# A decoder layer's first attention, with relative positions: groups over four query tiles, bias applied as a factor, operand rows made by 0/1 matmuls

## What is computed

```python
idx = jnp.arange(s)
dist = jnp.clip(idx[None, :] - idx[:, None], -R, R) + R      # R = 64
pe_k = rel_emb_k[dist]
pe_v = rel_emb_v[dist]
q, k, v = (qkv[0], qkv[1], qkv[2])
q = q / jnp.sqrt(jnp.asarray(hd, x.dtype))
score = jnp.einsum('bhqd,bhkd->bhqk', q, k) + jnp.einsum('bhqd,qkd->bhqk', q, pe_k)
attn = jax.nn.softmax(score, axis=-1)
ctx = jnp.einsum('bhqk,bhkd->bhqd', attn, v) + jnp.einsum('bhqk,qkd->bhqd', attn, pe_v)
return ctx @ W_out + b_out
```

## Time and profile before

| | us |
|---|---|
| median of 3 runs | 554.8 (551.67 to 556.12) |
| the profiled execution | 553.47 |
| its span, first to last instruction | 551.6 |
| TensorE busy | 445.8 |
| VectorE busy | 343.0 |
| ScalarE busy | 264.6 |
| GpSimd busy | 56.4 |
| mean granted TensorE clock | 0.849 |

### The profile page before, as it was taken

One profiled execution on the slowest core, in us unless ns is written; L12 is line 12 of the kernel. 1 busy time (PEld: TensorE's weight loads), 2 busy tenths in 40 slices (PEclk: granted clock), 3 DMA queues, 4 the chain that ended last, 5 costly groups with the idle time before them and its releaser, 6 DMA issues.

```text
span 551.6 us, 17721 instructions
## 1 busy us (share of the span) xinstructions
PE 445.8 (81%) x7898; PEld 277.8 (50%) x7898; DVE 343.0 (62%) x703; ACT 264.6 (48%) x547; POOL 56.4 (10%) x71
## 2 busy tenths in 40 slices
PE   0504777999999999899999757398899999878995
PEld 0300524777787877778988646242222222263452
DVE  3698465887666566465222206679688989165586
ACT  1700213555555464645656623135887878655211
POOL 1793000000000000000000007006200000000011
PEclk9855555999989797978897957588899999999999
DMA  8999993000000000000000150101800000000000
GB/s 159 165 206 310 163 295 61 2 4 4 4 4 4 4 4 4 4 4 4 6 4 5 41 163 4 36 1 37 193 1 2 2 0 1 2 1 0 1 15 24
DMA packets 18437, 26.81 MB, mean 49 GB/s; under 512 B 2688, under 2 KB 15256, under 8 KB 17832
## 3 DMA queue, kind: packets, MB, share of 16 engines
q1 hardware_dynamic: 16841, 19.38, 15.8%
q0 software_dynamic: 1520, 6.30, 4.9%
HBM read 16.68 MB, written 8.44 MB: 46 GB/s over the span
## 4 chain that ended last, share of the span: by engine, by line
PE 61%; DVE 13%; DMA 11%; ACT 8%; issue 4%; SPq 1%; POOLq 0%; POOL 0%; ACTq 0%; DVEq 0%
PE ps L1013 7%; PE ps L1050 7%; PE ps L1030 6%; PE ps L1001 6%; PE ps L1262 5%; PE ps L1312 5%; PE ps L980 4%; PE ps L1249 4%; DMA scr<-ctxT 4%; PE ps L1061 3%; DMA q_op<-neg_mT 2%; ACT crel L507 2%; DVE m_qk L849 2%; PE ps L1231 2%; DMA scr<-rel_v 2%
## 5 line engine op out<-in xcount | busy, mean ns | idle before, releaser
L700 DVE TENSOR_REDUCE m_qk<-ps 128x1 f32<-128x512 f32 x128 | 85.0, 687 | 47.8 <-PE ps L980 46.1
L980 PE MATMUL ps<-k_op,q_op 112*128 112x512 bf16 x128 | 60.1, 478 | 31.8 <-DMA k_op<-scr 23.3
L849 DVE TENSOR_REDUCE m_qk<-ps 128x2 f32<-128x1024 f32 x64 | 75.0, 1218 | 10.7 <-PE ps L1231 10.6
L487 ACT ACTIVATE band<-ps 128x512 f32<-128x512 f32 x64 | 38.2, 596 | 83.4 <-PE ps L1013 83.4
L1013 PE MATMUL ps<-q_op,rel_k 112*128 112x32 bf16 x1024 | 69.9, 235 | 5.8 <-DMA rel_k<-scr_rel 4.3
L611 ACT ACTIVATE band<-ps 128x512 f32<-128x512 f32 x128 | 66.9, 593 | 13.7 <-PE ps L1249 13.7
L1013 PEld LDWEIGHTS ps<-q_op,rel_k 112*128 112x128 bf16 x1024 | 63.4, 117 | 15.2 <-DMA q_op<-scr 4.8
L743 DVE TENSOR_TENSOR band<-ps,band 128x512 f32<-128x512 f32 x64 | 43.8, 684 | 36.3 <-PE ps L1030 29.5
L1030 PE MATMUL ps<-q_op,k_op 113*128 113x64 bf16 x1024 | 56.6, 204 | 4.2 <-issue 1.9
L1030 PEld LDWEIGHTS ps<-q_op,k_op 113*128 113x128 bf16 x1024 | 46.3, 105 | 18.0 <-issue 7.6
L524 ACT ACTIVATE p_out<-ps 128x512 f32<-128x512 f32 x64 | 38.2, 597 | 29.2 <-PE ps L1050 28.5
(11 more groups left out here) (202 smaller groups left out, 607.4 us busy)
## 6 DMA issues: line engine op xcount, KB each, us to landing
q_op<-in_zeros SPq DMA_DIRECT2D x2, 1024.0 KB
scr<-band SPq DMA_DIRECT2D x2, 768.0 KB, 10.8
scr<-rel_v SPq DMA_DIRECT2D x2, 768.0 KB, 10.1
...
```

Of the source, the lines that this page charges most:

```text
L700: dve.tensor_reduce(m_qk[:, tt, 8 * e + p:8 * e + p + 1], ps[:, bank, :], AX_X, ALU.max).then_inc(sm["m_done"], 1)
L849: dve.tensor_reduce(m_qk[:, IT * b + it, 2 * p:2 * p + 2], ps[:, 2 * (su % 2):2 * (su % 2) + 2, :], AX_X, ALU.max).then_inc(sm["rmax_done" ...
L980: i = pe.matmul(ps[:, bank, :], q_op[0:PR, e, p, tt * P:tt * P + P], k_op[0:PR, 0, p, b * S:b * S + S], start=True, stop=True)
```

## The change

The first attention is written anew; the rest stays, apart from where tiles lie in memory.

- A group u is one strip of 32 queries out of each of the four query tiles of a batch (8 groups of 128 queries). q_op's columns are permuted so that a group's are contiguous. For one offset x in the strip the window of relative keys is the same in all four tiles.
- Bias: the matmul for one x takes 8 pairs x 4 (or 3) tiles as columns, over 49 rows, once for even and once for odd heads at rows 0 and 64. ScalarE exponentiates it into eb; scores are exponentiated by themselves; GpSimd multiplies the near part of the exponentials by exp(bias). The near keys of a query are its own tile and the one on the nearer side.
- Far keys no longer have operands of their own. v_sb has seven blocks of 9 columns, so that 27 weight columns carry the values of one class in one of three places, the far classes in rows 9 to 26 of each 32. fin multiplies those by exp(far bias minus the relative maximum) and adds the three.
- Two separate maxima, of the relative scores and of q·k, enter as operand rows 48 and 49.
- Operand rows come from three bf16 parts by matmuls with a 0/1 matrix loaded from DRAM (sel), over strips of 32 rows, in place of the way through scr. In the rotary attention too sel is loaded rather than written by GpSimd, and its picks take 32 rows.
- The order is a list, relative_plan: step t, a rank in the step, a kind. Each engine runs through it. Banks 4 to 6 are a ring for all that ScalarE empties, banks 0 to 3 two pairs for VectorE, bank 7 holds PV.
- The transposes and the division move from the finish into each group (fin, back).
- Constants of the rotary attention and w_conv are loaded at the start, the MLP's weights after the last product with exp(bias).

Instructions of TensorE in the first attention, by source (a float32 matmul counted once):

| | before | after |
|---|---|---|
| bias | 1,024 of 112 rows, 32 columns | 1,024 of 49 rows, 32 or 24 columns |
| scores | 1,024 of 113 rows, 64 columns | 512 of 50 rows, 128 columns |
| maxima | 128 of 112 rows, 512 columns | 128 of 48 rows, 512 columns |
| PV | 1,024, 9 weight columns, 64 columns | 1,152, 27 weight columns, 32 to 96 columns |
| relative values | 1,024, 32 columns | 1,024, 32 or 24 columns |
| their addition | 256 of 8 rows, 64 columns | 512 of 128 rows, 32 columns |
| picks | none | 99 of 16 or 32 rows, 512 columns |

The core of the diff:

```diff
+GROUP = 11
+QK_BANKS = ((2, 3), (7, 0))
+V_BANKS = (1, 7)
+PAIR_BANKS = (slice(2, 4), slice(0, 2))
+PICK_ORDER = ((0, 2), (1, 3), (4, 6), (5, 7))
...
+def side(u):
+    return -1 if u % IT < IT // 2 else 1
+def second(u):
+    return (1 if side(u) < 0 else 0), IT - 1
+def regions(u, jt):
+    lo, hi = (jt, jt + 1) if side(u) < 0 else (jt - 1, jt)
+    parts = [(max(lo, 0), min(hi, IT - 1), 0), (0, lo - 1, 2), (hi + 1, IT - 1, 1)]
+    return [(a, z - a + 1, c) for a, z, c in parts if z >= a]
...
+def relative_plan():
+    plan = [(-1, 0, "relk", 0, 0)]
+    for n, k in enumerate((0, 1, 2)):
+        plan.append((-1, 1 + n, "pick", 0, k))
+    for k, t in ((3, 0), (4, 1), (5, 2), (6, 3), (7, 4)):
+        plan.append((t, 3, "pick", 0, k))
+    plan.append((2, 4, "v1", 0, 0))
+    for k in range(8):
+        plan.append((5 + k, 3, "pick", 1, k))
+    plan.append((12, 3.5, "zero", 0, 0))
+    for u in range(NT):
+        t = GROUP * u
+        plan += [(t + j, 1, "rel", u, j) for j in range(3)]
+        plan += [(t + 3 + p, 1, "max", u, p) for p in range(PAIRS)]
+        plan += [(t + 5, 4, "rel_rows", u, 0), (t + 6, 4, "factors", u, 0), (t + 13, 4, "qk_rows", u, 0)]
+        plan += [(t + 8 + q, 5, "bias", u, q) for q in range(4)]
+        plan += [(t + 16 + GROUP * p // PAIRS, 2, "scores", u, p) for p in range(PAIRS)]
+        plan += [(t + 24 + 2 * g, 6, "pv", u, g) for g in range(4)]
+        plan += [(t + 25 + 5 * f, 7, "crel", u, f) for f in range(2)]
+        plan += [(t + 27 + 5 * f, 8, "add", u, f) for f in range(2)]
+        plan += [(t + 33, 9, "ctx", u, 0), (t + 34, 1.5, "fin", u, 0), (t + 37, 9, "back", u, 0)]
+    return [(kind, u, n) for _, _, kind, u, n in sorted(plan, key=lambda x: x[:2])]
...
+of_act = {"relk": 1, "pick": 2, "rel_rows": 1, "qk_rows": 1, "bias": 2, "scores": 2, "crel": 1, "back": 1}
...
+sp.dma_start(ident[:, :], t["ident"]).then_inc(sm["ld_id"], 16)
+sp.dma_start(w_qkv[:, :], t["w_qkv"]).then_inc(sm["ld_wq"], 16)
+sp.dma_start(cols[:, :], t["cols"]).then_inc(sm["ld_wq"], 16)
+sp.dma_start(sel[:, :, :, :], t["sel"]).then_inc(sm["ld_sel"], 16)
+for u in range(2):
+    sp.dma_start(relk_f[HD * u:HD * u + HD, :], t["relk_ext"]).then_inc(sm["ld_rel"], 16)
+sp.dma_start(rows[:, :, :], bass.AP(t["rows"].tensor, 0, [[0, P], [1, 7 * D]])).then_inc(sm["ld_w"], 16)
+sp.dma_start(rel_v[:, :], bass.AP(t["relv_ext"].tensor, 0, [[HD, P], [1, 384 * HD]])
+             ).then_inc(sm["relv_ready"], 16)
+sp.dma_start(w_out[:, :], t["w_out"]).then_inc(sm["ld_w"], 16)
...
-zeros = lambda r, n: bass.AP(t["zeros"].tensor, 0, [[0, r], [1, n]])
-sp.dma_start(k_op[PR:PR + 1, :, :, :].rearrange("o a b c -> o (a b c)"), t["ones"]).then_inc(sm["ld_one"], 16)
...
+for kind, u, n in plan:
+    if kind in ("rel_rows", "qk_rows"):
+        k, arrived = ((0, rel_row), (1, qk_row))[kind == "qk_rows"]
+        sp.wait_ge(sm["bank_free"], ring[(kind, u, n)] + 1)
+        sp.dma_start(q_op[KR + k:P:64, :, col0(u):col0(u) + P], neg_mT[:, k, u % 2, :]
+                     ).then_inc(sm[arrived[u % 2]], 16)
...
+pool.memset(v_sb[:, :, :, :].rearrange("p t h w -> p (t h w)"), 0.0).then_inc(sm["v_clear"], 1)
+pool.wait_ge(sm["ld_wq"], 32)
+pool.tensor_scalar(w_qkv[:, 0:D], w_qkv[:, 0:D], Q_SCALE, None, ALU.mult).then_inc(sm["wq_ready"], 1)
...
+for kind, u, p in plan:
+    if kind == "scores":
+        n = PAIRS * u + p
+        first, tiles = second(u)
+        pair_of = arena[:, 1024 * (n % RING):1024 * (n % RING) + 1024]
+        beside = (P if side(u) > 0 else XW)
+        on0 = bass.AP(pair_of.tensor, pair_of.offset, [pair_of.ap[0], [512, 2], [P + XW, IT], [1, XW]])
+        on1 = bass.AP(pair_of.tensor, pair_of.offset + beside, [pair_of.ap[0], [512, 2], [P + XW, tiles], [1, XW]])
+        pool.wait_ge(sm["bank_free"], ring[(kind, u, p)] + 2)
+        pool.tensor_tensor(on0, on0, eb0[u % 2][:, p], ALU.mult)
+        pool.tensor_tensor(on1, on1, eb1[u % 2][:, p], ALU.mult).then_inc(sm["scaled"], 1)
...
+if kind == "bias":
+    which, xg = divmod(n, 2)
+    for e in range(2):
+        bank = emptied(kind, u, n, e)
+        if u >= 2:
+            act.wait_ge(sm["scaled"], PAIRS * (u - 1))
+        dst, tiles = ((eb0, IT), (eb1, IT - 1))[which]
+        act.activation(dst[u % 2][:, :, e, :, 16 * xg:16 * xg + 16],
+                       ps[:, bank, 0:16 * PAIRS * tiles].rearrange("y (x a i) -> y a i x", x=16, a=PAIRS), ACT.Exp
+                       ).then_inc(sm["bank_free"], 1)
+if kind == "scores":
+    k = PAIRS * u + n
+    if k == PAIRS:
+        act.wait_ge(sm["v_ready"], 3)
+    for e in range(2):
+        bank = emptied(kind, u, n, e)
+        if k >= RING:
+            v, p = divmod(k - RING, PAIRS)
+            act.wait_ge(sm["pv_done"], 4 * v + p // 2 + 1)
+            act.wait_ge(sm["bank_full"], ring[("crel", v, p // 4)] + 1)
+        act.activation(p_ring[:, k % RING, e, :], ps[:, bank, :], ACT.Exp).then_inc(sm["bank_free"], 1)
+if kind == "crel":
+    bank = emptied(kind, u, n)
+    if u >= 1:
+        act.wait_ge(sm["crel_added"], 2 * (u - 1) + n + 1)
+    act.activation(crel[:, n, :, :, :], ps[:, bank, 0:256].rearrange("r (x h i) -> r h i x", x=8, h=8), ACT.Identity
+                   ).then_inc(sm["bank_free"], 1)
...
+for b in range(B):
+    cs = slice(b * S, b * S + S)
+    done = []
+    for n in range(2):
+        dve.wait_ge(sm["first_part"], 2 * b + n + 1)
+        done.append(counted(dve.scalar_tensor_tensor(rest_of[n][b], ps[:, QK_BANKS[b][n], :], cols[:, C_BQ + n:C_BQ + n + 1],
+                                                     parts[n][:, 0, cs], ALU.add, ALU.subtract)))
+    for n in range(2):
+        dve.wait_ge(sm["dve"], done[n])
+        done.append(counted(dve.tensor_copy(parts[n][:, 1, cs], rest_of[n][b])))
+    for n in range(2):
+        dve.wait_ge(sm["dve"], done[2 + n])
+        dve.tensor_tensor(parts[n][:, 2, cs], rest_of[n][b], parts[n][:, 1, cs], ALU.subtract).then_inc(sm["split_done"], 1)
...
+dve.wait_ge(sm["factor_ready"], u + 1)
+one = counted(dve.tensor_tensor(lo, got[:, :, :, VW:2 * VW], fac(0), ALU.mult))
+two = counted(dve.tensor_tensor(hi, got[:, :, :, 2 * VW:3 * VW], fac(1), ALU.mult))
+dve.wait_ge(sm["dve"], one)
+three = counted(dve.tensor_tensor(lo, lo, got[:, :, :, 0:VW], ALU.add))
+dve.wait_ge(sm["dve"], three)
+dve.tensor_tensor(lo, lo, hi, ALU.add).then_inc(sm["pair_free"], 1)
+dve.wait_ge(sm["pair_free"], k + 1)
+link(dve.reciprocal(rsum[:, u % 2, :], below[:, :, HD]))
+rs = rsum[:, u % 2, :]
+dve.tensor_tensor(by_e(xn[:, u, :], HD), lo[:, :, :, 0:HD],
+                  bass.AP(rs.tensor, rs.offset, [rs.ap[0], [PAIRS, 2], [1, PAIRS], [0, HD]]), ALU.mult
+                  ).then_inc(sm["ctxn_ready"], 1)
...
+def bank_of(kind, u, n, k=0):
+    use = ring[(kind, u, n)] + k
+    if use >= 3:
+        pe.wait_ge(sm["bank_free"], use - 2)
+    return 4 + use % 3
...
+if kind == "pick":
+    of_k, two = picks_of(n)
+    pe.wait_ge(sm["split_done"], 2 * u + of_k + 1)
+    into = [bank_of(kind, u, n, k) for k in range(2)]
+    for part in range(3):
+        for bank, p in zip(into, two):
+            r = slice(32 * (p // 2), 32 * (p // 2) + 32)
+            i = pe.matmul(ps[:, bank, :], sel[r, 3 * of_k + part, p % 2, :], parts[of_k][r, part, u * S:u * S + S],
+                          start=(part == 0), stop=(part == 2))
...
+if kind == "bias":
+    if n == 0:
+        pe.wait_ge(sm[rel_row[u % 2]], 16 * (u // 2 + 1))
+    which, xg = divmod(n, 2)
+    it0, tiles = ((0, IT), second(u))[which]
+    delta = (0, side(u))[which]
+    into = [bank_of(kind, u, n, e) for e in range(2)]
+    for xx in range(16):
+        xi = 16 * xg + xx
+        w = P * delta - (XW * (u % IT) + xi) + ZERO
+        c = col0(u) + XW * it0 + xi
+        for e in range(2):
+            i = pe.matmul(ps[:, into[e], xx * PAIRS * tiles:(xx + 1) * PAIRS * tiles], rel_k[64 * e:64 * e + KR + 1, w:w + P],
+                          q_op[64 * e:64 * e + KR + 1, :, c:c + XW * (tiles - 1) + 1:XW], start=True, stop=True)
+            if xx == 15:
+                i.then_inc(sm["bank_full"], 1)
+if kind == "scores":
+    if n == 0:
+        pe.wait_ge(sm[qk_row[u % 2]], 16 * (u // 2 + 1))
+    into = [bank_of(kind, u, n, e) for e in range(2)]
+    for jt in range(IT):
+        for e in range(2):
+            i = pe.matmul(ps[:, into[e], jt * P:jt * P + P], k_op[64 * e:64 * e + KM, n, b * S + jt * P:b * S + jt * P + P],
+                          q_op[64 * e:64 * e + KM, n, col0(u):col0(u) + P], start=True, stop=True)
+            if jt == IT - 1:
+                i.then_inc(sm["bank_full"], 1)
+if kind == "pv":
+    if u == 0 and n == 0:
+        pe.wait_ge(sm["pv_zero"], 1)
+        pe.wait_ge(sm["v_ready"], 3)
+        pe.wait_ge(sm["v_ones"], 3)
+    if u >= 1 and n == 0:
+        pe.wait_ge(sm["ctx_ready"], u)
+    pe.wait_ge(sm["scaled"], PAIRS * u + 2 * n + 2)
+    for jt in range(IT):
+        for it0, tiles, c in regions(u, jt):
+            for hh in range(4):
+                a, e = divmod(hh, 2)
```

(34 more changed lines are left out.)

821 lines of the change are left out of this document (323 added, 498 removed).

## The result

| | us |
|---|---|
| kernel before, median of 20 runs | 554.75 |
| changed kernel, median of 20 runs | 555.24 |
| ratio, with its 95% interval | 1.0081 (1.0045 to 1.0118) |
| the changed kernel's profiled span | 552.6 |

The forecast was 491. The kernel takes as long as the one before. The medians differ by 0.5 us; the ratio compares only the runs within 1.5% of each kernel's fastest, and is not the ratio of the medians. The page's engine totals of the changed kernel answer.

What follows compares the result with a forecast made beforehand. TensorE was taken to bound the loop, something else the opening. Step 24 at 72 us, 166 to step 88, then 19, 13, 5 and a 10.5 finish gave 285 instead of 347, 62 us less: 491 us, range 450 to 526.

Steps and rivals of the forecast that it cites:

- The steady group: First attention's loop: each group of 11 steps takes 28.5 us, of which 20.1 is TensorE work.
- step 88: First attention's plan: reached at 238 us, 166 us after step 24; the steps after it lack maxima and bias.
- The waits: Each group in the loop: TensorE waits 6.3 us for banks and ScalarE.
- The bias handovers: Where bias stands behind scores or scores behind bias: TensorE waits about 0.95 us less what lies between.
- The wait of the final transposes: Step 1 of a group: they wait 1.7 us for ScalarE's two exponentials and the 512-column context copy.
- The tail: End of first attention: steps 88 to 99 take 19 us, the last PV, relative values and addition 13.
- The opening: Start of first attention: products start at 11 to 15 us, step 12 at 54, step 24 at 72.
- The pair of picks: Opening: a pair cycles in 1.65 us, 0.65 of it three concurrent products; 16 pairs take 26.4 us.
- Rotary attention costed at nothing: After the first attention: rotary attention and MLP issue the same work, so no time is added.
- rival 2: Loop's bias pairs don't overlap, 57 ns each: 29 us more, 520 us; chance 0.13.
- rival 4: PV in the loop: 27 weight columns cost 51 ns a record, 76 us more, 567 us; chance 0.05.
- the other side: PV's three times wider weights make the kernel slower, 567 us; chance 0.05.

Runs made afterwards that it cites:

- series 5 of the probe: TensorE alone, no kernel: 512 float32 products, 27 weight columns, 64 columns over four strips (PV form); 28.1 us, 27.4 ns a record.
- series 3: TensorE alone, no kernel: 1,024 bf16 products of 49 rows over two row strips, 24 columns (bias form); 27.4 us, 26.8 ns a record.
- the padded kernel before: Kernel before with half its relative-value products cut in two along their columns, 1,024 records more; 593.26 us, ratio 1.0740.

## Why the prediction was wrong

**The steady group, 28.5 us forecast, 32.4 measured.** Over the 5.8 groups between first PV and step 88 this is 23 of the 63 us. The failed step is the way in which prices became a sum: PV at 18 ns a record, relative values and their addition at 15. Those are burst prices. They were read from series of 16 to 128 records in the earlier trace rows, and a series of up to 128 is what one block carries without a gap. The group issues 901 records (4,503 in five groups); at 28 to 31 ns they take 25 to 28 us, where the sum had 20.1 for its work. Relative values, PV and addition alone are 672 of them, priced at 11.0 us and worth 19 to 21. The trace of before had the warning: 240 us for 6,719 records, 35.7 ns each; a gap of 0.97 us, put down to issue, at 130.04 in the middle of a bias block; and 29.4 ns a record from 259 to 319 us, near the loop's end. The busy share was read as a TensorE that is busy with bias blocks and scores. The old loop has 840 records in an eighth, the new group 901, at 35.7 and 36.0 ns. That a group's time goes with its records is shown by the records added and removed; why both averages lie above the supply's 29 is shown for the new loop alone, by its bank waits.

**The waits, 6.3 us a group.** This step held in kind and roughly in size. The bias handovers were forecast at 0.7 to 0.95 us each, and the trace has 14.2 us in twenty, 0.71 each. The wait of the final transposes was forecast at 1.7 a group; it is 1.3 (6.3 us in five, factor and context copy together), and 1.5 once the bias blocks are moved. With the scores' 0.5 the waits are 4.6 us a group, 1.7 less than forecast, and TensorE is busy for 24.3 where the sum had 22.2. So the waits were known. What was wrong is that they were taken as what the design costs: moving four blocks and four transposes in the plan gave 14 and 9.4 us.

**The tail, 32 us forecast, 49.1 measured.** It is the same mis-sized term without cover. Steps without maxima and bias were priced at 19 us and the last PV at 13, by burst prices. The tail's 1,435 records at 28 to 31 ns are 40 to 44 us, and its gaps put down to issue are 13.6 us, 8.0 of them in four gaps ahead of PV.

**The opening, first PV at 72 forecast, 83.1 measured.** Its start held: the q and k products begin at 13.70 us, within the 11 to 15, behind a memset that took 6.8 by the element as assumed. The pair of picks failed: 1.65 us forecast, 2.1 to 2.3 measured in either form, 7 to 11 us for the 16 pairs. The step that failed is the clock: three 512-column products were priced at full clock (0.65), where a pair at that clock took 1.59 us in all, and at half they take 1.46 by themselves. Picks over 128 rows brought the clock to 0.85 but not the time, since six products then follow each other.

**Rotary attention costed at nothing.** The forecast saw that its picks go one behind the other over 32 rows, but not what such picks do to the clock. This was 9.9 of the 11.3 us, of which 8.8 came back with 128 rows, and the edit alone costs the kernel before 13 us.

**What held.** Bias pairs overlap: 32 weight loads in 0.75 us at 145.54, so the pair price of rival 2 was rightly left out. PV does not cost by its 27 weight columns: 72 weight loads in 0.94 us at 288.83, and series 5 of the probe costs what series 3 does, so rival 4 falls. GpSimd's products took 0.73 and 0.60 us, against 0.77 and 0.61. The finish took 12.4 instead of 15. The prediction calls the 2.45 us of the earlier trace rows the time of two casts; it is that of one, and nothing in the sum rests on it. No forecast rival was the one that came: the other side had a price for wide weights, not one for a record as such.

```profile
145.54 0.75 PEld L1044 LDWEIGHTS ps<-q_op,rel_k 49*128 49x128 bf16 x32 [1.01 <-ACT arena L504]
```

**What stays open.** What TensorE waits for in the gaps, beyond their rate and the packet counts. Why the granted clock of the loop is 0.79 instead of the old loop's, with picks of either form (0.81 with 128 rows). And what part of the 40 us in the padded kernel before is clock. Neither of these two was tried alone.
